# A one-core decoder layer: the last routed block of each token part is found ahead of the routed loop, and the row gathers start one pair of blocks earlier

## The reference, cut to what matters

```python
logits = flat @ gate_w.T
probs = jax.nn.softmax(logits, axis=-1)
_, top_idx = jax.lax.top_k(logits + expert_bias, 2)
top_w = jnp.take_along_axis(probs, top_idx, axis=-1)
top_w = top_w / jnp.sum(top_w, axis=-1, keepdims=True)
combine = jnp.sum(jax.nn.one_hot(top_idx, 16) * top_w[..., None], axis=1)
for e in range(16):
    out = out + combine[:, e:e + 1] * _swiglu(flat, w_gate[e], w_up[e], w_down[e])
out = out + _swiglu(flat, sw_gate, sw_up, sw_down)
x = _layernorm(x + out)
```

## Time and profile before

| | |
|---|---|
| three runs, median (lowest to highest) | 661.34 us (659.74 to 663.22) |
| the profiled execution: time, and span | 660.12 us, 658.4 us |
| busy share of the span: PE, PEld, DVE, ACT, POOL | 95%, 75%, 81%, 69%, 72% |
| mean granted clock of TensorE | 0.988 |

### The profile page before, as it was taken

How to read it: one execution, slowest core, us unless ns; L and a number is a source line. 1 busy time by engine, 2 the same in 40 slices (tenths; PEclk the granted TensorE clock), 3 DMA queues, 4 the chain that set the end, 5 groups by cost and what they waited for, 6 DMA issues and landing times.

```text
span 658.4 us, 12041 instructions
## 1 busy us (share of the span) xinstructions
PE 626.1 (95%) x3545; PEld 492.5 (75%) x3545; DVE 531.7 (81%) x852; ACT 453.6 (69%) x742; POOL 476.4 (72%) x456
## 2 busy tenths in 40 slices
PE   8989999999999999999999999999999989899980
PEld 6677888878888788888887888878888877555540
DVE  5999999999999999999999999976973547622346
ACT  3768788797887978879788788786422455433364
POOL 3386989879898798887987889677752573855554
PEclk9999999999999999999999999999999999999995
DMA  4162113111131111311212112043034287359554
GB/s 163 54 262 79 65 50 112 53 59 64 48 112 64 48 64 48 112 64 48 79 41 104 64 48 105 6 129 102 17 100 123 68 243 287 94 159 272 168 129 143
DMA packets 25993, 66.66 MB, mean 101 GB/s; under 512 B 4099, under 2 KB 16899, under 8 KB 23179
## 3 DMA queue, kind: packets, MB, share of 16 engines
q1 hardware_dynamic: 23131, 58.54, 26.5%
q0 software_dynamic: 2832, 7.75, 4.7%
HBM read 58.00 MB, written 9.85 MB: 103 GB/s over the span
## 4 chain that ended last, share of the span: by engine, by line
PE 82%; DVE 6%; POOL 4%; issue 3%; ACT 2%; DMA 2%; POOLq 0%; ACTq 0%; DVEq 0%
PE ps L878 38%; PE ps L892 9%; PE ps L908 7%; PE ps L893 4%; PE ps L1172 4%; PE ps L810 3%; PE ps L828 3%; DVE conv L1744 2%; PE ps L1221 2%; PE ps L852 2%; POOL conv L752 1%; PE ps L917 1%; PE ps L918 1%; POOL conv L668 1%; PE ps L1146 1%
## 5 line engine op out<-in xcount | busy, mean ns | idle before, releaser
L1744 DVE SCALAR_TENSOR_TENSOR conv<-ps,w_raw,conv 128x506 f32<-128x506 f32 (+3 forms) x352 | 320.6, 934 | 15.3 <-ACT conv L1386 9.2
L878 PE MATMUL ps<-x_hi,w_hi 128*128 128x512 f32 x384 | 158.8, 414 | 2.1 <-DVE conv L1744 1.1
L1386 ACT ACTIVATE conv<-ps,w_raw 128x512 f32<-128x512 f32 x160 | 108.2, 687 | 64.4 <-PE ps L878 63.9
L878 PE MATMUL ps<-x_hi,w_lo 128*128 128x512 f32 x384 | 151.7, 395 | 0.0
L878 PE MATMUL ps<-x_lo,w_hi 128*128 128x512 f32 x384 | 150.7, 392 | 0.0
L525 POOL TENSOR_TENSOR decay<-cum_b,cum_tok 128x512 f32<-128x512 f32 (+1 forms) x128 | 103.3, 828 | 9.4 <-DMA cum_b<-cum_scratch 9.4
L878 PEld LDWEIGHTS ps<-x_hi,w_hi 128*128 128x128 f32 x384 | 72.6, 189 | 20.2 <-issue 2.4
L531 POOL TENSOR_TENSOR decay<-decay,mask 128x512 f32<-128x512 f32 x64 | 82.7, 1292 | 5.0
L878 PEld LDWEIGHTS ps<-x_hi,w_lo 128*128 128x128 f32 x384 | 72.5, 189 | 16.8
L878 PEld LDWEIGHTS ps<-x_lo,w_hi 128*128 128x128 f32 x384 | 72.9, 190 | 12.7
L1371 ACT ACTIVATE conv<-conv 128x1024 f32<-128x1024 f32 x80 | 79.3, 1059 | 1.5 <-DVE conv L1744 1.5
(11 more groups left out here) (285 smaller groups left out, 1090.0 us busy)
## 6 DMA issues: line engine op xcount, KB each, us to landing
cum_b<-cum_scratch SPq DMA_DIRECT2D x16, 1024.0 KB, 4.7
w_raw<-in_winT SPq DMA_DIRECT2D x15, 778.0 KB, 4.3
y_all<-in_wgu SPq DMA_DIRECT2D x4, 1408.0 KB, 11.9
late<-in_wdn SPq DMA_DIRECT2D x2, 1408.0 KB
x_scratch<-conv SPq DMA_DIRECT2D x19, 128.0 KB, 4.9
late<-in_woutT SPq DMA_DIRECT2D x1, 2048.0 KB, 9.2
ys_scratch<-y_blk SPq DMA_DIRECT2D x32, 64.0 KB
res_scratch<-conv SPq DMA_DIRECT2D x11, 130.0 KB
```

Source lines behind the costliest of these rows:

```text
L878: mm = pe.matmul(ps[:, tile_bank(n, tile) + hf, :], wp[:, par, w], xp[:, kk, t], start=(i == 0), stop=(i == 5))
L1386: act.activation(conv[:, par, tile, hf * 512:(hf + 1) * 512], ps[:, tile_bank(n, tile) + hf, :], ACT.Copy, scale=w_raw[:, par, tap:tap + 1 ...
L1744: dve.scalar_tensor_tensor(out=o[:, :, s:], in0=u[:, :, 0:T - s], scalar=w_raw[:, par, c:c + 1], in1=o[:, :, s:], op0=ALU.mult, op1=ALU.ad ...
```

## The change

`AHEAD` goes from 4 to 6, so six block gathers stand ahead of the loop and the last one is issued in pair 27 (before: pair 29). The residual adds on POOL around the loop's start are re-ordered to fit. `NPAIRED` = 9: row gathers 1 to 9 are tied to pairs 29, 31 and 33 (before: 1 to 6 to pairs 31 and 33).

The four last-block numbers are worked out by `blocks_by_part` on DVE just ahead of the loop, from `slot`, `tok_x` and `valid` in sorted order, and PE turns them in pair 15 (`SEEN_AT` = 15). The slots that the row gathers use as indices are copied in the loop, for token blocks 0 to 2 in pair 19 and for 3 to 7 in pair 29 (`slots_of_picks`, a wait each on `ld_res` and the new `ld_res2`); POOL waits for them by the new `v_slot`.

DVE's `weights_of_picks` moves up within pair 31, ahead of that pair's `take_hidden`, and the three `weigh_low` of token blocks 0 to 2 follow it there. The first `weigh_high` moves into pair 33, between its two `gate_block`. Two waits on `v_valid` become a link wait in the earlier stage.

```diff
-SEEN_AT = TBS + 17
+SEEN_AT = TBS + 4
+NPAIRED = 9
-AHEAD = 4
+AHEAD = 6
...
                 elif j == 3:
                     add_residual(TBS - 4)
+                elif j == 4:
+                    add_residual(TBS - 3)
+                    add_residual(TBS - 2)
+                elif j == 5:
+                    add_residual(TBS - 1)
             for j in range(AHEAD, NBLK, 2):
                 i = TBS + j - AHEAD
                 in_pair(i, 0)
                 gather_block(j)
-                if j == AHEAD:
-                    add_residual(TBS - 3)
-                elif j // 2 - AHEAD // 2 <= TB:
+                if j > AHEAD:
                     in_pair(i, 1)
                     gather_res(j // 2 - AHEAD // 2 - 1)
                 in_pair(i, 2)
                 gather_block(j + 1)
-                if j == AHEAD:
-                    add_residual(TBS - 2)
-                    add_residual(TBS - 1)
...
-                if n < 6:
+                if n < NPAIRED:
                     in_pair(ITEMS - AHEAD + n // 3 * 2, n % 3)
...
                 pool.wait_ge(S["y_seen"], pool.value_load(last_blk[n:n + 1, 0:1], min_val=1, max_val=NBLK))
                 pool.tensor_tensor(part_seen[:, n:n + 1], zero[:, :], zero[:, :], ALU.add)
+                pool.wait_ge(S["v_slot"], 1 if hi <= HOISTED else 2)
...
-                if i == SEEN_AT + 1:
-                    pe.wait_ge(S["v_blk"], NPART)
+                if i == SEEN_AT:
+                    pe.wait_ge(S["v_blk"], 1)
                     pe.transpose(ps[0:NPART, i % 2, 2 * P:3 * P], part_f, ident[:, :])
...
+            def blocks_by_part():
+                vlink(dve.tensor_scalar(seen_a, slot, 6, NE - 1, ALU.logical_shift_right, ALU.bitwise_and),
+                      dve.tensor_scalar(seen_b, slot, 7, None, ALU.logical_shift_right),
+                      *[dve.scalar_tensor_tensor(out=part_in[:, n, :], in0=tok_x, scalar=float(P * (lo or hi)), in1=valid,
+                                                 op0=ALU.is_ge if lo else ALU.is_lt, op1=ALU.mult)
+                        for n, (_, lo, hi) in enumerate(PICK_PARTS)])
                 vlink(dve.scalar_tensor_tensor(out=seen_c, in0=seen_b, scalar=float(NE), in1=seen_b,
                                                op0=ALU.is_ge, op1=ALU.mult))
+                vlink(dve.tensor_tensor(seen_f.rearrange("p k j -> p (k j)"), seen_a, seen_c, ALU.max))
+                vlink(*[dve.tensor_tensor(part_blk[:, n, :], part_in[:, n, :], seen_f[:, kk, :], ALU.mult)
+                        for n, (kk, _, _) in enumerate(PICK_PARTS)])
+                dve.tensor_reduce(part_f, part_blk, AX.X, ALU.max).then_inc(S["v_blk"], 1)
+            def slots_of_picks(lo, hi):
+                if lo == 0:
+                    dve.wait_ge(S["ld_res"], 16 * HOISTED)
+                else:
+                    dve.wait_ge(S["ld_res2"], 16 * (TB - HOISTED))
+                dve.tensor_copy(slot_t.rearrange("p (k b) -> p k b", k=PICKS)[:, :, lo:hi],
+                                res_tok[:, lo:hi, D:D + 2].rearrange("p b k -> p k b")).then_inc(S["v_slot"], 1)
...
+            blocks_by_part()
             for i in range(TBS, ITEMS, 2):
                 gate_block(i)
+                if i == ITEMS - 2:
+                    weigh_high(0)
                 gate_block(i + 1)
+                if i == PICK_AT + 2:
+                    weights_of_picks()
+                    for b in range(HOISTED):
+                        weigh_low(b)
                 if i + 2 < ITEMS:
                     take_hidden(i)
                     take_hidden(i + 1)
-                if i + 1 == SEEN_AT:
-                    blocks_of_picks()
-                if i == PICK_AT + 2:
-                    weights_of_picks()
-            for b in range(HOISTED):
-                weigh_low(b)
-            for b in range(LEADING):
+                if i == TBS + 8:
+                    slots_of_picks(0, HOISTED)
+                if i == TBS + 18:
+                    slots_of_picks(HOISTED, TB)
+            for b in range(1, LEADING):
                 weigh_high(b)
```

More of the change, by code:

```diff
@@ L225, in build_layer @@
         slot_t = take(PICKS * TB).bitcast(I32)
-        seen_a, seen_b, seen_c = (take(PICKS * TB).bitcast(I32) for _ in range(3))
-        seen_f = take(PICKS * TB).rearrange("p (k b) -> p k b", k=PICKS)
+        seen_a, seen_b, seen_c = (take(PICKS * TBS).bitcast(I32) for _ in range(3))
+        seen_f = take(PICKS * TBS).rearrange("p (k j) -> p k j", k=PICKS)
+        part_in, part_blk = (take(NPART * TBS).rearrange("p (n j) -> p n j", n=NPART) for _ in range(2))
         part_f, part_seen, part_top = (take(NPART) for _ in range(3))
@@ L270, in build_layer @@
                  "ld_wo ld_xt ld_ctx ld_id ld_rt o0 r0 s0 q0 n0 s2 q2 n2 a_link "
-                 "p_const v_own s_xrank v_link v_xin p_xpb v_xis s_xtab v_xtok v_xeid v_valid st_x1 "
+                 "p_const v_own s_xrank v_link v_xin p_xpb v_xis s_xtab v_xtok v_xeid st_x1 "
                  "a_wo v_wo a_yh v_yl p_yl yh_done oh_done a_oh ld_early eo_done v_ve v_root p_root xt1 a_xg hx_done a_sx v_gx gt_done a_gx o1 r1 s1 q1 n1 n1p t1 a_t1 "
@@ L274, in build_layer @@
                  "ld_sh ld_gu ld_dn ld_copy st_x2 st_res ld_res a_el "
-                 "tx_done a_xt gu_done a_s a_u p_h v_h ht_done a_ht v_ht dn_done a_y p_res v_mix st_out y_seen v_blk v_lb ys_set n2a")
+                 "tx_done a_xt gu_done a_s a_u p_h v_h ht_done a_ht v_ht dn_done a_y p_res v_mix st_out y_seen v_blk v_lb ys_set n2a v_slot ld_res2")
         S = {n: sem(n) for n in names.split()}
@@ L688, in gather_res @@
                                         bass.IndirectOffsetOnAxis(ap=slot_x[:, b:b + 1], axis=0)
-                                        ).then_inc(S["ld_res"], 16)
+                                        ).then_inc(S["ld_res" if b < HOISTED else "ld_res2"], 16)
             def add_residual(i):
@@ L1634, in _ @@
                     act.preload_act_table_set("natural_log_exp_and_others")
-                    act.wait_ge(S["ld_res"], 16 * TB)
+                    act.wait_ge(S["ld_res"], 16 * HOISTED)
+                    act.wait_ge(S["ld_res2"], 16 * (TB - HOISTED))
                     act.activation(e_pick, res_tok[:, :, D + 2:D + 4].rearrange("p b k -> p k b"), ACT.Exp).then_inc(S["a_el"], 1)
@@ L1903, in tokens_by_id @@
                                          op0=ALU.mult, op1=ALU.add).then_inc(S["v_xtok"], 1)
-                dve.tensor_copy(valid, tab_x[:, 2 * TBS:3 * TBS]).then_inc(S["v_valid"], 1)
-                dve.tensor_scalar(no_slot, tab_x[:, 2 * TBS:3 * TBS], -float(NGRP * G), float(NGRP * G), ALU.mult, ALU.add
-                                  ).then_inc(S["v_valid"], 1)
+                vlink(dve.tensor_copy(valid, tab_x[:, 2 * TBS:3 * TBS]),
+                      dve.tensor_scalar(no_slot, tab_x[:, 2 * TBS:3 * TBS], -float(NGRP * G), float(NGRP * G),
+                                        ALU.mult, ALU.add))
             dve.wait_ge(S["ld_xt"], 16)
@@ L2070, in last_of_picks @@
             def last_of_picks():
-                vlink(dve.tensor_reduce(part_top[0:NPART, 0:1], ps[0:NPART, (SEEN_AT + 1) % 2, 2 * P:3 * P], AX.X, ALU.max))
+                vlink(dve.tensor_reduce(part_top[0:NPART, 0:1], ps[0:NPART, (SEEN_AT) % 2, 2 * P:3 * P], AX.X, ALU.max))
                 dve.tensor_scalar(last_blk[0:NPART, :], part_top[0:NPART, 0:1], 1.0, None, ALU.add
```

10 lines of the change are left out of this document (removed).

## The result

The changed kernel takes 656.36 us in the median (654.80 to 656.40), against 661.34. The ratio is 0.9916, with an interval of [0.9891, 0.9942]: about 5.6 us less, between 3.8 and 7.2. The forecast was 3.55 us less, 657.8. The direction was right, the size too small: the median lies 0.5 under the forecast's own range, which began at 656.9. (One execution, of 2,219 us, was disturbed and stands outside this range and the ratio.)

The account below looks back on a forecast made before the run. The prediction took PE to bound the loop and POOL's row gathers the end. A 3.85 us gain from earlier gathers less 0.3 for a later loop start gave 3.55: 661.34 to 657.8 us, range 655.8 to 660.8.

Parts of the forecast that it names:

- the forecast's own range: Median time if the main forecast of 657.8 us holds: from 656.9 to 658.2 or so, chance 0.57.
- the pairs as long as now: Routed loop: a sign that would show the forecast, its pairs keeping their length; no gain counted.
- They do not delay it, and later gathers come earlier than now: POOL ahead of the loop: two added block gathers and three moved adds do not delay the gather at 572.27.
- queue term: POOL's time from pair 33's first gate product to the last row gather; 18.01 us before, forecast to shrink by 3.85.
- The row gathers: POOL's queue at the loop's end: the last row gather comes at 646.95 instead of 650.82, gain 3.85 us.
- gather 9 waits for the last transposes: POOL in pair 33: the ninth row gather waits for PE's transposes, ending at 637.70, and comes at about 638.0.
- The start of the loop: Ahead of the loop: `blocks_by_part` on DVE slows POOL beside it, loop 0 to 0.86 us later; 0.3 taken.
- The rule that I weighed: GpSimd shares SBUF interfaces with VectorE and contends with some DVE instructions; taken in full, the gain becomes 3.0 us.
- DVE's work in pairs 31 and 33: Weighings moved into the loop, three `weigh_low` (1.27 us) and one `weigh_high` (1.16), cost nothing if their rows land in time.
- a DVE instruction taken from there frees nothing by itself: Tail after the loop: POOL's row gathers set the end, so removing DVE work there gains nothing.
- All three rivals: Gain partly given back, 658.8 to 659.4 us (0.27); nothing gained, 661.3 (0.09); slower, DVE held or 20 blocks needed, 664.1 (0.07).

Follow-up runs that it names:

- deeper gathers alone: Kernel before with six block gathers ahead of the loop instead of four and the residual adds re-ordered: 658.68 us, ratio 0.9941.
- more transfers: A 512 KB copy added behind each of the seven weight loads: 665.56 us in the kernel before (ratio 1.0054), 661.17 us in the changed kernel (0.9990).
- deeper gathers of the fourth set: The kernel before with six block gathers ahead and re-ordered adds, run again in another set on one chip: 659.45 us, ratio 0.9970.
- two loads: Kernel before with five of seven expert weight copies left out: 659.55 us, again 660.36; with six block gathers ahead as well, 658.58.
- before again: The kernel before, unchanged, profiled and timed again: 662.25 us, ratio 0.9998.

## Why the prediction was right or wrong

**The step that failed** is "the pairs as long as now", with the sentence on the added block gathers, "They do not delay it, and later gathers come earlier than now", to which I gave no gain. The loop became 1.52 us shorter in the profiled pair of executions, and deeper gathers alone gain 2.0 to 3.9 us with the queue term unchanged. I had read the steady stretch as PE's because PE was busy 42.77 of 43.50 us and never asked what the other 0.73 was. In the profile of before, the second half of the first pair takes 3.54 us and four pairs take 5.66, 5.46, 5.67 and 5.80, where after has 3.21, 5.38, 5.35, 5.35 and 5.36; these differences add up to 1.5. The lengths of the pairs were there to be compared.

**How much is shown.** That deeper gathers, with the re-ordered adds that go with them, bring a gain by themselves is shown by the kernel that has them alone, on two chips. With four ahead and all loads PE waits for blocks gathered inside the loop in three of four profiles (1.6, 1.3 and, with more transfers, 4.2 us); with six or eight no profile has such a row, and deeper gathers of the fourth set had a landing of 6.3 us and no wait. That the weight loads lengthen landings rests on three profiles with two loads, with medians of 3.2 to 3.3 where those with all seven, and nothing added, give 3.7 to 4.2. The added transfers did not lengthen the median, 3.8 in before and 3.5 in after. Leaving loads out may also have brought the block stores forward; no run tells the two apart.

The first pair of profiles shows less of this cause. PE's transposes of gathered blocks in the profile of before, a plain pair's (598.74) among them:

```profile
576.93 0.44 PE L1146 MATMUL ps<-ident,xb 128*128 128x128 f32 x2 [0.35 <-DMA xb<-x_scratch,y_all]
...
598.74 0.66 PE L1146 MATMUL ps<-ident,xb 128*128 128x128 f32 x4
...
604.20 0.76 PE L1146 MATMUL ps<-ident,xb 128*128 128x128 f32 x4
...
631.26 0.77 PE L1146 MATMUL ps<-ident,xb 128*128 128x128 f32 x4
```

The wait at 576.93 is for the fourth gather, at 572.27. Both kernels issue it ahead of the loop; it landed 4.6 us after its issue before and 3.8 after. So that 0.3 of the 1.5 us is not the work of `AHEAD`. The pairs of 5.67 and 5.80 us, 0.8 together, have transposes 0.1 us longer, as if their second block had only just landed: a late block is likely there, not shown. In the pairs of 5.66 and 5.46, 0.4 together, the transposes ran as in a plain pair, and the cause stays open.

**The row gathers** were right: 3.93 us for 3.85. Every gather came 0.6 to 1.5 us earlier than the forecast time, mostly because the loop had become shorter. Counted from pair 33's first gate product the last one is at 14.08 against 646.95 - 632.81 = 14.14, and the sixth and the ninth agree within 0.1. One detail I cannot confirm: that gather 9 waits for the last transposes. They end at 636.26 and it comes 0.36 later, which fits; but it is also three steps of 1.25 behind the sixth, which followed the count of 19 blocks at 632.17. The two limits have met within a tenth. What the edits share of the 3.9: the first part's earlier count some 1.8, the ties the rest; each of the two kernels that have only one of them has a queue term of 15.9.

**The start of the loop** was charged 0.3 and cost nothing there. POOL's add took 0.74 as in the earlier trace rows, in after and with the new work doubled. The rule that I weighed (Trainium skill, GPSIMD Engine Reference, section Specifications) says that POOL and DVE contend. Around the new instructions no run shows a price on POOL's side; DVE's took 3.67 us for an estimate of 2, and PE did not feel it. Nor did a gather beside `weigh_low` become longer: the one at 631.05 took 0.95, beside the weighings of 630.68 to 631.96.

**DVE's work in pairs 31 and 33** was right at nothing, and "a DVE instruction taken from there frees nothing by itself" too: putting the weighings back changes nothing that can be measured. One reading was wrong without weight in the sum: the `weigh_high` at 639.73 is that of the second 128 tokens; before, the first ran from 637.31 to 638.47.

**The sum.** 3.93 for 3.85, 0 for -0.3, and 1.5 or more for 0: in the profiled execution 5.3 against 3.55. All three rivals looked for losses. None asked whether the loop itself could become shorter.

## What to carry to other kernels

A loop in which an engine is 98% busy may still hide a microsecond or more: compare the lengths of its iterations, and ask of the long ones what came late. When a change prefetches one step deeper, price what the prefetch covers and not only what it costs; take more than one execution, since a late transfer strikes in some and not in others. When the clock falls behind a stall of PE, the stall costs more than itself. And ask which other transfers, stores for one, free what the loop waits for.

## What the runs showed of the hardware

- A block gather of 128 rows lands 2.7 to 6.1 us after its issue in one and the same kernel (median 3.7, before again), with weight loads in flight beside it.
- PE idle for 1.6 us was followed by a granted clock of 0.61 over 3.80 us, with gate products about 0.58 us apart instead of 0.30 (before again). Not every such wait was: in before with more transfers, waits of 1.25 and 1.38 us left the granted clock at 1.00 (599.60 to 604.00, 606.80 to 611.00), and after the third, of 1.56, it was 0.58 from 615.30 to 618.00.
- In the kernel with the new DVE work twice, one DVE instruction on 22 elements took 0.18 us at 571.99 and 0.65 at 575.11, and a group of four on 11 elements took 1.41 at 569.89 and 0.40 at 573.84. The long one of each two ran beside adds or a product of POOL, which kept their lengths (0.57 and 0.74).
